# Deformable-sampling kernel: offsets of a batch loaded by eight transfers instead of four, x ahead of y on semaphores of their own

## What is computed

```python
off = conv2d(x, ow, ob).reshape(Bn, K, 2, Hh, Ww)          # K = 9 taps, y and x offsets
cy = iy[None, None, :, None] + dy[None, :, None, None] + off[:, :, 0]
cx = ix[None, None, None, :] + dx[None, :, None, None] + off[:, :, 1]
y0 = jnp.floor(cy); x0 = jnp.floor(cx); wy = cy - y0; wx = cx - x0
samp = gather(y0i, x0i, (1 - wy) * (1 - wx)) + gather(y0i, x0i + 1, (1 - wy) * wx) \
     + gather(y0i + 1, x0i, wy * (1 - wx)) + gather(y0i + 1, x0i + 1, wy * wx)
out = jnp.einsum('bckhw,ock->bohw', samp, w.reshape(w.shape[0], Cin, K))
h = jax.nn.relu(group_norm1(deform_conv(x, w1, b1, ow1, ob1), g1, be1)) + x
h = jax.nn.relu(group_norm1(deform_conv(h, w2, b2, ow2, ob2), g2, be2)) + h
```

## Time and profile before

| what | value |
|---|---|
| median of 3 runs | 729.74 us (726.46 to 733.1) |
| the profiled execution | 729.7 us |
| its span in the trace | 727.5 us |
| busy shares of the span | PE 79%, DVE 82%, ACT 62%, POOL 20% |
| DMA queues' share of 16 engines | q0 (issued by GpSimd) 35.8%, q1 (by SyncE) 9.7% |

### The profile page before, as it was taken

One profiled execution on the slowest core, in us unless ns is written; L12 is line 12 of the kernel. 1 busy time (PEld: TensorE's weight loads), 2 busy tenths in 40 slices (PEclk: granted clock), 3 DMA queues, 4 the chain that ended last, 5 costly groups with the idle time before them and its releaser, 6 DMA issues.

```text
span 727.5 us, 29228 instructions
## 1 busy us (share of the span) xinstructions
PE 576.0 (79%) x13258; PEld 413.8 (57%) x13258; DVE 600.2 (82%) x853; ACT 453.1 (62%) x803; POOL 146.1 (20%) x258
## 2 busy tenths in 40 slices
PE   2719999999888698888886788669888888659491
PEld 1205887775654477666665454357666666537380
DVE  6998999942459999999998443999999999884866
ACT  2776774233227789999983412669999899251514
POOL 1005000010241343344200025134334420000000
PEclk9959999999988899999999798979999999969696
DMA  5004000000669898888730066979888862000003
GB/s 215 0 9 109 4 5 20 4 5 20 168 219 386 246 310 276 277 276 274 247 130 2 3 178 216 379 235 306 279 287 283 279 222 112 3 1 5 1 4 116
DMA packets 30198, 111.16 MB, mean 153 GB/s; under 512 B 11140, under 2 KB 15940, under 8 KB 25976
## 3 DMA queue, kind: packets, MB, share of 16 engines
q0 software_dynamic: 14912, 87.85, 35.8%
q1 hardware_dynamic: 15160, 21.42, 9.7%
HBM read 92.25 MB, written 19.65 MB: 154 GB/s over the span
## 4 chain that ended last, share of the span: by engine, by line
DVE 38%; PE 36%; DMA 10%; ACT 6%; issue 5%; SPq 2%; POOL 1%; DVEq 0%; ACTq 0%; POOLq 0%
PE psum L1433 12%; DVE arena L820 8%; DVE arena L822 7%; DVE arena L823 7%; DMA arena<-offsets_by_batch 7%; PE psum L1487 6%; PE psum L1642 6%; DVE arena L812 3%; PE psum L1521 3%; ACT arena L1212 2%; PE psum L1451 2%; PE psum L1652 2%; DMA offsets_by_batch<-offsets 1%; PE psum L1391 1%; SPq L520 1%
## 5 line engine op out<-in xcount | busy, mean ns | idle before, releaser
L1521 PE MATMUL psum<-arena 64*64 64x297 f32 (+4 forms) x4512 | 223.1, 340 | 48.3 <-DVE arena L823 40.9
L1521 PEld LDWEIGHTS psum<-arena 64*64 64x64 f32 x4512 | 171.1, 136 | 106.8 <-DVE arena L823 49.6
L1737 POOL DMA_DIRECT2D arena<-offsets_by_batch x128 | 78.1, 624 | 200.0 <-DVE arena L823 130.1
L1239 ACT ACTIVATE arena<-psum 128x396 f32<-128x396 f32 (+1 forms) x192 | 86.1, 509 | 36.4 <-PE psum L1521 24.0
L1487 PE MATMUL psum<-arena 32*32 32x512 f32 x2304 | 88.3, 651 | 22.7 <-issue 16.9
L820 DVE SCALAR_TENSOR_TENSOR arena<-arena 128x396 f32<-128x396 f32 (+1 forms) x192 | 98.2, 554 | 3.5 <-ACT arena L1226 2.5
L1433 PE MATMUL psum<-arena 32*32 32x512 f32 x2592 | 93.6, 597 | 0.0
L822 DVE SCALAR_TENSOR_TENSOR arena<-arena 128x792 f32<-128x792 f32 (+3 forms) x96 | 92.3, 961 | 0.0
L823 DVE SCALAR_TENSOR_TENSOR arena<-arena 128x792 f32<-128x792 f32 (+3 forms) x96 | 92.2, 960 | 0.0
L1545 PE MATMUL psum<-arena 64*64 64x256 f32 x1152 | 83.1, 381 | 2.6 <-ACT arena L1242 2.2
L1487 PEld LDWEIGHTS psum<-arena 32*32 32x32 f32 x2304 | 49.3, 107 | 59.3 <-issue 44.9
(11 more groups left out here) (169 smaller groups left out, 640.8 us busy)
## 6 DMA issues: line engine op xcount, KB each, us to landing
arena<-offsets_by_batch POOLq DMA_DIRECT2D x112, 576.0 KB, 7.9
arena<-offsets_by_batch POOLq DMA_DIRECT2D x16, 624.0 KB, 7.6
offsets<-arena SPq DMA_DIRECT2D x32, 256.0 KB, 10.0
offsets_by_batch<-offsets SPq DMA_DIRECT2D x184, 24.0 KB
arena<-columns POOLq DMA_DIRECT2D x24, 160.0 KB, 9.3
columns<-arena POOLq DMA_DIRECT2D x8, 320.0 KB, 6.7
arena<-in_x SPq DMA_DIRECT2D x4, 512.0 KB, 5.3
out<-arena SPq DMA_DIRECT2D x8, 256.0 KB, 2.2
```

Source lines behind the costliest of these rows:

```text
L1239: ins = a.activation(ap(to + half * 2 * K * SX, [[SR, 2], [SX, 2 * K], [1, w]]), ap_ps(bank, [[CH, 2], [w, 2 * K], [1, w]], half * 2 * K * ...
L1521: ins = t_.matmul(ps_t(s, bank + r, first * K * w, many * K * w), window, ap(g_at(unit, d0) + first * TW + s * w, [[GS + TW, many], [SLOTS ...
L1737: g.dma_start(cols(in_at(n, 0), 2 * in_rows(n) * W, 64 * r + 32 * half, 32), bass.AP(batch_d.tensor, 2 * (4 * r * NB + n) * INS, [[0, QW / ...
```

## The change

Each of the four transfers of a batch load carried the x and the y offsets of 32 partitions in one row of each. It is cut in two: four transfers bring the x offsets, then four bring the y offsets. The x transfers add to one semaphore, the y transfers to another. `distances` waits for x alone. The first y term of a batch (unit 0) waits for y, and the other two follow it in ScalarE's order. Both semaphores count as the one did, 64 for each batch.

```diff
--- before.py
+++ after.py
@@ -289,7 +289,7 @@
         s_cv, s_cve = sem("offset_products_ready"), sem("offsets_written")
         s_d1 = sem("offsets_bounded")
         s_ds = [sem(f"bounded_offsets_stored_{m}") for m in range(4)]
-        s_in = [sem(f"offsets_loaded_{i}_of_three") for i in range(3)]
+        s_in = [[sem(f"{axis}_offsets_loaded_{i}_of_three") for axis in "xy"] for i in range(3)]
         s_ar = [sem(f"offsets_arranged_{i}_of_four") for i in range(4)]
         s_u, s_nd, s_g = sem("offset_distances_ready"), sem("y_terms_ready"), sem("tent_products_ready")
         s_un, s_se = sem("samples_ready"), sem("samples_copied")
@@ -1214,13 +1214,15 @@
 
             def distances(L, n):
 
-                act.wait_ge(s_in[n % 3], in_count(L, n))
+                act.wait_ge(s_in[n % 3][0], in_count(L, n))
                 tx = cols(in_at(n, 0), in_rows(n) * W)
                 a.activation(tx, tx, ACT.Abs, bias=con("minus_q")).then_inc(s_u, 1)
 
             def y_terms(L, unit):
 
                 n, u = divmod(unit, NU)
+                if u == 0:
+                    act.wait_ge(s_in[n % 3][1], in_count(L, n))
                 if unit >= RING:
                     act.wait_ge(s_un, UNITS * L + unit - RING + 1)
                 a.activation(ap(g_at(unit, 1), [[TW, KR], [1, 2 * WB[u]]]),
@@ -1732,12 +1734,13 @@
                 pool.wait_ge(s_ar[n % 4], arranged(L, n))
                 if n >= 3:
                     pool.wait_ge(s_g, UNITS * L + NU * (n - 2))
-                for half in range(2):
-                    for r in range(2):
-                        g.dma_start(cols(in_at(n, 0), 2 * in_rows(n) * W, 64 * r + 32 * half, 32),
-                                    bass.AP(batch_d.tensor, 2 * (4 * r * NB + n) * INS,
-                                            [[0, QW // 2], [2 * NB * INS, 4], [1, 2 * in_rows(n) * W]])
-                                    ).then_inc(s_in[n % 3], 16)
+                for axis in range(2):
+                    for half in range(2):
+                        for r in range(2):
+                            g.dma_start(cols(in_at(n, axis), in_rows(n) * W, 64 * r + 32 * half, 32),
+                                        bass.AP(batch_d.tensor, 2 * (4 * r * NB + n) * INS + axis * in_rows(n) * W,
+                                                [[0, QW // 2], [2 * NB * INS, 4], [1, in_rows(n) * W]])
+                                        ).then_inc(s_in[n % 3][axis], 16)
 
             for pair in (1, 3):
                 for ch in range(NCH):
```

## The result

The changed kernel takes 719.38 us (median of 6 runs, 717.25 to 723.73), the kernel before 729.62 us (6 runs): ratio 0.9871 [0.9832, 0.9911]. Run again beside the first experiments it gave 719.0 us against 730.87, ratio 0.9834 [0.9787, 0.9882]. So it gains 10 to 12 us, or 1.3 to 1.7%. The forecast was 725.6 us with a range down to 721.5.

The account below looks back on a forecast made before the run. It took VectorE to bound the sampling stage, with 6.6 us of waits for ScalarE. Gains of 1.74 + 0.64 + 0.78 + 0.98 = 4.14 us took 729.7 us to 725.6 us, range 721.5 to 730.5.

Parts of the forecast that it names:

- What bounds the stage: Middle of the first sampling pass: VectorE busy 104.99 of 107.60 us, so loads can return only its waits, 6.6 us.
- Distances need x alone, and x now comes first in the queue: Batch loads: x lands some 6 us earlier, at worst 3 us, so ScalarE's steady waits ahead of its distances go.
- the 222.07 allowed: Batch 0, first pass: latest landing of y, in us, that lets L812 start 1.74 us earlier.
- The sum of 4.14 us: VectorE's gains over both sampling passes: 1.74 + 0.64 + 0.78 + 0.98 us.
- The 1.74 us at the start: Batch 0, first pass: L812 starts 1.74 us earlier, right behind L459; 0.8 us at worst.
- The waits behind loads: VectorE's waits behind ScalarE's load waits: gains 0.64 us (batch 4), 0.78 (batches 9, 11), 0.98 (second pass, batch 11).
- the change leaves these: VectorE's other sampling waits, 2.5 us, have no load wait of their size ahead and stay; ScalarE is itself nearly full.
- the fuller gain: Rival, chance 0.15: ScalarE catches up, all 6.6 us of VectorE's waits close, 723.1 us.
- What it adds: 128 more GpSimd issues, 2.2 us a load, 71 us in all, hidden; further rows 2.6 us; VectorE pays nothing.
- the estimate of 10 ns: Price of each packet on the data queues, solved from their shares; 4096 further rows make 41 engine-us.
- neither slower one: Two rivals, chance 0.04 each: transfers with their own price, 813 us; VectorE held up by issuing, at most 801 us.
- transfers with a price of their own: Slower rival, chance 0.04: a load's landing grows with its number of transfers; y 3.2 us late, 813 us.

Follow-up runs that it names:

- Joined waits: Changed kernel's eight transfers, x ahead of y, but the distances wait for both semaphores, so for the whole load: 720.27 us, 0.9846 of the kernel before.
- the wide ones: Four transfers of 64 partitions by 9 KB for a load, x first: 806.76 us, 1.1023 of the kernel before; with distances waiting for both semaphores 801.4 us, 1.0966.
- the hybrid with four transfers in its first batches: Kernel before with eight transfers only in batches 3 to 15 of each pass, distances waiting for all eight: 721.68 us, 0.9883 of the kernel before.
- the other hybrid: Kernel before with eight transfers only in batches 0 to 2 of each pass, distances waiting for all eight: 725.72 us, 0.9939 of the kernel before.
- telling the row in two: Kernel before, its four transfers each written as 32 partitions by two 9 KB rows in place of one 18 KB row: 730.56 us, 1.0025.
- rows apart: Loads read the input image, each partition its own row; against the kernel before: four of 64 partitions 1.1112, four of 32 partitions 1.3395, eight (distances wait for all) 1.048.
- by image: Batch loaded by eight transfers of one image each (16 partitions, every fourth of a group's 64, by 18 KB), one semaphore: 1.0612 of the kernel before.

## Why the prediction was wrong

**What bounds the stage:** right. VectorE bounds sampling, and what the sampling stages gave back (6.7 us) is the size of its waits there.

**"Distances need x alone, and x now comes first in the queue":** this is the step that failed. The facts in it are right (x of batch 0 at 214.7 us against 215 foretold; y at 218.9, before the 222.07 allowed), but the gain doesn't hang on it. Joined waits and y ahead of x give the same time. By the traces early x carries at most some 2 of the 10 us, and by the medians 1.3 (720.27 - 719.0), which is no more than scatter. The cause is the cut of the transfers: the whole load ends 1.0 us sooner (10.6 us from its issue in place of 11.6), and what stands behind it lands sooner too. I had priced the cut as pure cost (2.2 us of issue, 2.6 us of packets over the run) and asked only how late y would be, never whether all eight might land before the four had. The row that could have warned me was the earlier trace rows with the earlier trace rows: engines 45.5% busy over the run with both queues, and a landing of 7.9 us for 576 KB, left room for a load to be moved sooner.

**The sum of 4.14 us:** too small. The 1.74 us at the start came (1.8). The waits behind loads came too, but "the change leaves these", said of the other 2.5 us, was wrong: the fuller gain, given 0.15, was what VectorE's waits did, 6.6 to 0.3 us. It came with every load landing sooner, also those that ScalarE had not been seen to wait for, so these runs do not tell whether early x alone would have closed them. That ScalarE is busy nine tenths of the stage did not keep it from catching up. The price of the fuller gain, 723.1 us, was still 3.7 us too high, about the part outside sampling.

**Outside sampling nothing was foretold,** and 3.8 us came. 2.3 us lie in the second pass's convolution of offsets. TensorE's idle time ahead of those matmuls, before and after:

```profile
  issue: 61.8, 59
```

```profile
  issue: 58.0, 56
```

Most of these stops come 128 matmuls apart, and the profile names no engine for them. Whether the cut shortens this stretch is not shown, for it varies among all kernels. With loads of four transfers of 32 partitions it is 36.3 and 38.4 us, in the wide ones 38.8 to 41.1, in those cut by axis into eight throughout 34.0 to 35.1, and 34.7 in the one of 16 partitions by 18 KB, which loses. But the hybrid with four transfers in its first batches, whose loads in this stretch are those of before, has 33.1, and the other hybrid 31.6. That a transfer in the way holds up TensorE's instructions is a guess, and no run tests it. The 1.5 us behind the last batch are missing with y ahead of x (112.9 us), a kernel that keeps the whole gain, so they are hardly the cut's own. Both stay open.

**What it adds:** right, but for the packets. Issues of 0.567 us, no queue behind them late, L812 with the same median, 1354 ns, beside twice as many issues. Further packets were 10240 and not 4096: the 4096 rows of the sum, and 6144 packets of 4 bytes. A 4-byte packet took 9 ns, and cutting a row in two added 5 ns (2 x 347 - 689), so the estimate of 10 ns was near for the one and twice too high for the other. By the two shares q0's engine time did not rise at all (4142 against 4167 engine-us). A wait for y stands only at batch 0, 1.8 us, under VectorE's cover.

**The rivals:** neither slower one came in this change. But "transfers with a price of their own" is real in other cuts: sixteen cost 4.6%, and eight of 16 partitions 0.8%. The Trainium skill, page "DMA: Bandwidth & Descriptors", gives about 2.0 us fixed for each transfer (section "Anatomy of one DMA") and advises to coalesce many small ones (section "Rules for kernel authors"). Here eight of 288 KB beat four of 576 KB by 1.3 to 1.7%. Four more fixed parts one after another would have made a load end later, and it ended 1.0 us sooner, so they overlapped, as the rows before had hinted.

**Settled and open.** Shown: the cause is the cut of a load into transfers and not the order or the waits; the gain adds up over start and steady part; the number of transfers alone loses; and in the kernels that gain a load's packets come to 16 in flight sooner, in the one of 16 partitions by 18 KB later. Open: whether four transfers with rows' packets of 9 KB would gain as well, since telling the row in two did not make such packets; why the second set of 8 joins when it does; and why a packet takes up to 1.9 times as long in the loads that start with more than 8 in flight. No variant beat the changed kernel; its joined form is equal to it.

## What to carry to other kernels

When a transfer is cut in order to have one half early, cost the landing of the whole load and of what is queued behind it as well, and test with the wait joined again: one run tells order from shape. Where the engine that bounds a stage waits for a producer that is nearly full, don't count only the waits with a late load right ahead of them; take all of them as the upper end and give it more than 0.15. Before a load is made wider, look at how many of its packets are in flight and how long each takes: with 64 partitions in a transfer 15 were in flight after 1.5 us, but one of 9 KB took 631 ns in place of 347.

## What the runs showed of the hardware

- The same bytes through the same queue: q0 was busy 35.8% with four transfers of 32 partitions by 18 KB and 45.8% (of a longer span) with four of 64 by 9 KB, and the kernel took 10% longer.
- A row of a load was one packet, of 18, 9 or 4.6 KB, in all kernels. A row of 18 KB took 689 ns and one of 9 KB 347 ns in transfers of 32 partitions with shared rows; one of 9 KB took 631 ns in transfers of 64.
- A load started with 8 packets in flight in transfers of 32 partitions with shared rows, and with 4 in transfers of 16 partitions by 18 KB. With 64 partitions, with rows apart and by image it had 9 to 13 after 0.6 us and 14 to 16 after 1.5 us.
- DMA engines at a full share moved 230 to 265 GB/s from 278 to 376 us in those last cuts, while single microseconds of the changed kernel reached 404 in the mean over its loads.
- Giving each partition a row of its own in DRAM, in place of one read by sixteen, did not help: 1.111 against 1.105 of the kernel before, with 64 partitions in a transfer.
- Two rows that lie end to end in DRAM and on the partition were moved as one: the same 14912 packets on q0, and one of 18 KB for each row.
- VectorE's L812 took 1350 to 1357 ns with one of the loads' issues beside it and 1350 to 1355 ns without (tile of 128x2304, the kernel before), while the issues beside it took 772 ns in the median and the others 554.
